# Four changes to PSUM banks and queue orders in a chain of four spectral layers

## What is computed

```python
xs  = rfft2(x)                                   # over both image axes
o1  = relu(xs @ w1 + b1)                         # complex, 8 blocks of 48 channels
o2  = softshrink(o1 @ w2 + b2, 0.01)             # real and imaginary part each
out = irfft2(o2) + x
```

## Time and profile before

| | |
|---|---|
| median of 3 runs | 2125.78 us |
| the profiled execution | 2123.25 us |
| its span, first to last instruction | 2121.5 us |
| mean granted TensorE clock | 0.978 of full speed |
| TensorE matmuls busy | 91% of the span |
| VectorE, ScalarE, GpSimd busy | 55%, 48%, 21% |

### The profile page before, as it was taken

One profiled execution on the slowest core, in us unless ns is written; L12 is line 12 of the kernel. 1 busy time (PEld: TensorE's weight loads), 2 busy tenths in 40 slices (PEclk: granted clock), 3 DMA queues, 4 the chain that ended last, 5 costly groups with the idle time before them and its releaser, 6 DMA issues.

```text
span 2121.5 us, 68757 instructions
## 1 busy us (share of the span) xinstructions
PE 1933.5 (91%) x31104; PEld 1592.9 (75%) x31104; DVE 1175.4 (55%) x2480; ACT 1012.2 (48%) x1644; POOL 439.9 (21%) x425
## 2 busy tenths in 40 slices
PE   5899984688998999999999999999799999999996
PEld 4677762566766999999999999999577777777774
DVE  3686887877855433333333333332566666666674
ACT  3655645566753333333333333333566555555652
POOL 3211103875621110000000000000311211212100
PEclk9999997799999999999999999999999999999999
DMA  9424727407435111111111111114804457257314
GB/s 166 90 48 81 126 53 137 62 4 126 96 84 132 30 30 30 30 30 30 30 30 30 30 30 30 30 30 71 140 3 89 70 96 124 49 81 126 62 30 93
DMA packets 299699, 141.03 MB, mean 66 GB/s; under 512 B 275760, under 2 KB 298032, under 8 KB 299440
## 3 DMA queue, kind: packets, MB, share of 16 engines
q1 hardware_dynamic: 299440, 137.08, 35.2%
HBM read 74.14 MB, written 62.91 MB: 65 GB/s over the span
## 4 chain that ended last, share of the span: by engine, by line
PE 73%; DVE 15%; ACT 6%; issue 3%; DMA 1%; SPq 1%; POOL 1%; DVEq 0%; POOLq 0%; ACTq 0%
PE ps L659 19%; PE ps L644 19%; DVE u L886 7%; PE ps L558 7%; PE ps L495 6%; PE ps L509 6%; PE ps L573 5%; PE ps L526 5%; PE ps L476 4%; ACT z L698 3%; DVE st L923 2%; DVE clamp L880 2%; PE ps L537 1%; DVE xs L911 1%; PE ps L629 1%
## 5 line engine op out<-in xcount | busy, mean ns | idle before, releaser
L1035 DVE TENSOR_TENSOR gl<-g,gh 128x512 fp32r<-128x512 f32 x192 | 156.7, 816 | 476.9 <-ACT gh L824 476.9
L886 DVE TENSOR_TENSOR u<-ps,clamp 64x192 f32<-64x192 f32 (+1 forms) x864 | 375.4, 434 | 27.8
L821 ACT ACTIVATE g<-ps,colp 128x512 f32<-128x512 f32 x192 | 132.5, 690 | 529.6 <-PE ps L644 529.6
L495 PEld LDWEIGHTS ps<-const,z 128*48 128x48 f32 x8384 | 269.5, 125 | 108.7 <-issue 100.9
L698 ACT ACTIVATE z<-ps 64x512 f32<-64x512 f32 x366 | 234.5, 641 | 106.7 <-PE ps L476 99.8
L495 PE MATMUL ps<-const,z 128*48 128x64 f32 (+1 forms) x8384 | 272.2, 218 | 8.9 <-issue 4.1
L1122 POOL COPY xn<-xs 128x512 f32<-128x512 f32 x144 | 151.4, 1090 | 569.4 <-PE ps L476 389.7
L659 PE MATMUL ps<-w2h,gh 128*128 128x384 f32 x768 | 261.9, 341 | 0.0
L659 PE MATMUL ps<-w2h,gl 128*128 128x384 f32 x768 | 258.6, 337 | 0.0
L659 PE MATMUL ps<-w2l,gh 128*128 128x384 f32 x768 | 257.5, 335 | 0.0
L509 PE MATMUL ps<-zf,w 112*64 112x512 f32 (+2 forms) x992 | 246.5, 569 | 9.8 <-ACT zf L718 9.7
(11 more groups left out here) (70 smaller groups left out, 2451.2 us busy)
## 6 DMA issues: line engine op xcount, KB each, us to landing
after<-xs SPq DMA_DIRECT2D x96, 384.0 KB, 5.4
xs<-after SPq DMA_DIRECT2D x94, 384.0 KB, 8.7
after<-om SPq DMA_DIRECT2D x32, 384.0 KB, 4.3
out<-xs SPq DMA_DIRECT2D x32, 384.0 KB, 5.4
xm<-after SPq DMA_DIRECT2D x30, 384.0 KB, 6.3
xs<-in_x SPq DMA_DIRECT2D x24, 384.0 KB, 8.8
wstage<-in_spectral SPq DMA_DIRECT2D x16, 210.0 KB, 5.9
xs<-in_x SPq DMA_DIRECT2D x4, 768.0 KB, 11.6
```

Source lines behind the costliest of these rows:

```text
L495: mm = pe.matmul(ps[a * SIDE:a * SIDE + BLOCK, F2_BANK, n * L.kh:(n + 1) * L.kh], z[:, g % 2, slot, :], basis(col + a * SIDE, L.kh), start ...
L886: dve.tensor_tensor(u[to, g % 2, :, start + b:start + size:BATCH], whole, limited, ALU.subtract).then_inc(u_ready, 1)
L1035: dve.tensor_tensor(gl[:, n % 4, :], g[:, n % 2, :], gh[:, n % 4, :], ALU.subtract).then_inc(g_low, 1)
```

## The change

- `m2` writes to banks 4 and 7 in turn, and waits for the group before the last in place of the last one. Since VectorE's scratch `clamp` is now no longer guarded by that wait, VectorE waits itself for its own four subtractions before it clamps again.
- `f6` writes to bank 6 alone, and waits for the eviction of the one before. Only in the drains does it go to banks 6 and 0 in turn.
- ScalarE's fourth piece of an `f1` stands behind the column eviction in place of ahead of it, in full layers and in the norm layer.
- At the head of the norm layer VectorE does its six pieces of the lead-in ahead of three `centre` calls, which were first.

```diff
-def spread_before(g):
+def spread_of(count):
+    return sum(layer_of(g).spread for g, _ in GROUPS[:count])
+def drains(g, k):
+    last = [b for _, b in SEGMENTS if g < b][0]
+    return g == last - 1 or g == last - 2 and k >= layer_of(g).first_rows
+def row_bank(g, k):
+    return 1 if drains(g, k) and k % 2 else 0
+def rows_to_clear(g, k):
+    n = ROWCHUNKS * g + k
+    earlier = [m for m in range(n) if row_bank(*ROW_CHUNKS[m]) == row_bank(g, k)]
+    return earlier[-1] + 1 if earlier else 0
...
-        F1_BANKS, F6_BANKS = (0, 1), (6, 7)
-        F2_BANK, M1_BANK, M2_BANK, F5_BANK = 2, 3, 4, 5
+        F1_BANKS, M2_BANKS, F6_BANKS = (0, 1), (4, 7), (6, 0)
+        F2_BANK, M1_BANK, F5_BANK = 2, 3, 5
...
 TensorE, m2
                 pe.wait_ge(h_ready, n + 1)
-                if n >= 1:
-                    pe.wait_ge(u_ready, spread_before(g) + L.spread * t)
+                if n >= 2:
+                    pe.wait_ge(u_ready, spread_of(n - 1))
+                bank = M2_BANKS[n % 2]
 (norm layer)
-                before = (g - BLOCKS) * L.n + t
-                if before:
-                    pe.wait_ge(u_imag, BATCH * before)
+                if imag_of(n - 1):
+                    pe.wait_ge(u_imag, imag_of(n - 1))
 TensorE, f6
-                if n >= 2:
-                    pe.wait_ge(res_ready, n - 1)
+                clear = rows_to_clear(g, k)
+                if clear:
+                    pe.wait_ge(res_ready, clear)
 ScalarE, spectral
+                        f2(g, t)
                         for k in late:
                             f1(g + 1, k, PIECES[3:4])
-                        f2(g, t)
 VectorE, m2 of full layers
+                    if groups_before(g) + t:
+                        dve.wait_ge(u_ready, spread_of(groups_before(g) + t))
                     dve.tensor_scalar(part, data, LAMBDA, -LAMBDA, ALU.min, ALU.max).then_inc(clamped, 1)
 VectorE, spectral
+                for k in range(TWINS):
+                    f1(first, k)
                 if norm:
                     for n in range(CHUNKS, CHUNKS + AHEAD):
                         centre(n)
-                for k in range(TWINS):
-                    f1(first, k)
```

More of the change, by code:

```diff
@@ L98, in groups_before, with imag_of @@
     return sum(LAYER[n // BLOCKS].n for n in range(g))
-def spread_before(g):
-    return sum(LAYER[n // BLOCKS].n * LAYER[n // BLOCKS].spread for n in range(g))
+GROUPS = [(g, t) for g in range(LAYERS * BLOCKS) for t in range(LAYER[g // BLOCKS].n)]
+def spread_of(count):
+    return sum(layer_of(g).spread for g, _ in GROUPS[:count])
+def imag_of(count):
+    return sum(BATCH for g, _ in GROUPS[:count] if layer_of(g).norm)
+def drains(g, k):
+    last = [b for _, b in SEGMENTS if g < b][0]
+    return g == last - 1 or g == last - 2 and k >= layer_of(g).first_rows
+ROW_CHUNKS = [(g, k) for g in range(LAYERS * BLOCKS) for k in range(ROWCHUNKS)]
+def row_bank(g, k):
[4 more added lines that the diff above has]
+    return earlier[-1] + 1 if earlier else 0
 def shrunk_before(g):
@@ L245, in build @@
         ps = ctx.enter_context(nc.psum_tensor("ps", [P, 8, 512], F32))
-        F1_BANKS, F6_BANKS = (0, 1), (6, 7)
-        F2_BANK, M1_BANK, M2_BANK, F5_BANK = 2, 3, 4, 5
+        F1_BANKS, M2_BANKS, F6_BANKS = (0, 1), (4, 7), (6, 0)
+        F2_BANK, M1_BANK, F5_BANK = 2, 3, 5
         LAST_BANKS = (F5_BANK, M1_BANK)
-        LEAD_BANKS = (F1_BANKS, F6_BANKS, F1_BANKS)
+        LEAD_BANKS = (F1_BANKS, (6, 7), F1_BANKS)
         TURN_BANKS, MM1_BANKS, MM2_BANKS = (6, 7), (4, 5), (0, 1, 2, 3)
@@ L525, in m2 @@
                         col = READY_SECOND if start + c < SPAN else MINUS
-                        mm = pe.matmul(ps[b * SIDE:(b + 1) * SIDE, M2_BANK, p * PAIR:(p + 1) * PAIR],
+                        mm = pe.matmul(ps[b * SIDE:(b + 1) * SIDE, bank, p * PAIR:(p + 1) * PAIR],
                                        h[0:ROWS, n % 2, c * SIDE:(c + 1) * SIDE],
@@ L536, in m2 @@
                         col = READY_SECOND + a * BLOCK
-                        mm = pe.matmul(ps[a * SIDE:(a + 1) * SIDE, M2_BANK, q * BLOCK:(q + 1) * BLOCK],
+                        mm = pe.matmul(ps[a * SIDE:(a + 1) * SIDE, bank, q * BLOCK:(q + 1) * BLOCK],
                                        h[0:ROWS, n % 2, q * SIDE:(q + 1) * SIDE],
@@ L548, in f5 @@
                         pe.wait_ge(s_const, 16)
-                    pe.wait_ge(u_ready, spread_before(g + 1))
+                    pe.wait_ge(u_ready, spread_of(groups_before(g + 1)))
                     if L.norm:
-                        pe.wait_ge(u_imag, BATCH * L.n * (g - BLOCKS + 1))
+                        pe.wait_ge(u_imag, imag_of(groups_before(g + 1)))
                     if L.norm and g % BLOCKS < 2:
@@ L568, in f6 @@
                     pe.wait_ge(v_ready, CHUNKS * (g + 1))
-                if n >= 2:
-                    pe.wait_ge(res_ready, n - 1)
+                clear = rows_to_clear(g, k)
+                if clear:
+                    pe.wait_ge(res_ready, clear)
                 rows = slice(k * ROWCHUNK, (k + 1) * ROWCHUNK)
                 for a in range(2):
-                    mm = pe.matmul(ps[a * SIDE:(a + 1) * SIDE, F6_BANKS[n % 2], 0:ROWCHUNK * BLOCK],
+                    mm = pe.matmul(ps[a * SIDE:(a + 1) * SIDE, F6_BANKS[row_bank(g, k)], 0:ROWCHUNK * BLOCK],
                                    basis(C_D6 + a * SIDE, SIDE), v[:, g % 2, rows, :].rearrange("p h c -> p (h c)"),
@@ L747, in m2 @@
                 act.wait_ge(m2_done, groups_before(g) + t + 1)
+                bank = M2_BANKS[(groups_before(g) + t) % 2]
                 start, size = L.groups[t]
@@ L751, in m2 @@
                     act.activation(u[HALF:SIDE, g % 2, :, start + b:start + size:BATCH],
-                                   ps[part, M2_BANK, 0:size // BATCH * BLOCK].rearrange("p (s c) -> p c s", c=BLOCK),
+                                   ps[part, bank, 0:size // BATCH * BLOCK].rearrange("p (s c) -> p c s", c=BLOCK),
                                    ACT.Copy).then_inc(u_imag, 1)
@@ L878, in m2 @@
                     pairs = size // BATCH
-                    part, data = clamp[:, 0:pairs * PAIR], ps[:, M2_BANK, 0:pairs * PAIR]
+                    part, data = clamp[:, 0:pairs * PAIR], ps[:, bank, 0:pairs * PAIR]
+                    if groups_before(g) + t:
+                        dve.wait_ge(u_ready, spread_of(groups_before(g) + t))
                     dve.tensor_scalar(part, data, LAMBDA, -LAMBDA, ALU.min, ALU.max).then_inc(clamped, 1)
@@ L889, in m2 @@
                 for b in range(BATCH):
-                    data = ps[b * HALF:(b + 1) * HALF, M2_BANK, 0:size // BATCH * BLOCK]
+                    data = ps[b * HALF:(b + 1) * HALF, bank, 0:size // BATCH * BLOCK]
                     dve.tensor_copy(u[0:HALF, g % 2, :, start + b:start + size:BATCH],
@@ L910, in f6 @@
                 to = residual(g, k * ROWCHUNK, ROWCHUNK)
-                dve.tensor_tensor(to, ps[:, F6_BANKS[n % 2], 0:ROWCHUNK * BLOCK].rearrange("p (h c) -> p h c", c=BLOCK),
+                dve.tensor_tensor(to, ps[:, F6_BANKS[row_bank(g, k)], 0:ROWCHUNK * BLOCK].rearrange("p (h c) -> p h c", c=BLOCK),
                                   to, ALU.add).then_inc(res_ready, 1)
```

## The result

The kernel after takes 2096.76 us (median of 4 runs, 2094.48 to 2098.42), the kernel before, run beside it, 2125.87 us (4 runs, 2122.17 to 2129.84). The ratio is 0.9862, with a 95% interval of 0.9841 to 0.9883: faster by 1.4%, 29 us, against a forecast of 21 us. The time lies inside the whole range (2089 to 2123) and 0.2 us outside the forecast's own, which begins at 2097. The profiled execution has a span of 2092.7 us at a mean granted clock of 0.975, against 2121.5 us at 0.978.

What follows compares the result with a forecast made beforehand. The prediction took TensorE's waits (73% of the chain), or VectorE's work where that is the chain, as the bound. Terms -24 - 8 + 14.2 - 2.9 = -20.7 us from 2125.78 gave 2105.1 us; whole range 2089 to 2123, its own 2097 to 2114.

Steps and rivals of the forecast that it cites:

- A border gains 1.37 of 1.69 us: Borders of two blocks, layers 2 and 3: 1.37 of 1.69 us of waits go; with the head, 24 us in all.
- my new wait before `f6`: At a border, `f6` with one bank waits for its eviction: 0.25 us come back.
- The 0.45 us at `zf`: At a border, the column eviction starts earlier, taking about 0.45 us off the first mix's 0.52 us wait for `zf`.
- Layer 0: Waits at block borders and VectorE's idle 1.07 us at the last exit go: 8 us gained, bounds 4 and 14.
- the second rival: Full layers: the wait moves to VectorE, gains of 11 not 24 and 4 not 8; 2122 us, chance 0.14.
- Norm layer, fourth piece: The piece, now behind the column eviction, delays the next `f1` by about 1.1 us: 14.2 us lost, bounds 0 and 20.
- the fourteen waits that I listed as signs: Norm layer: fourteen idle times of about 1.5 us before `f1` were to show in the changed trace.
- The first rival: Norm layer: the fourth piece costs nothing, the wait being the queue's own; 2091 us, chance 0.13.
- The small rival with 2096 us: A sum like the forecast's, with a larger gain in the norm layer's lead-in; near 2096 us, chance 0.05.
- Norm layer, lead-in: Head of the norm layer: VectorE stays the chain and gains 2.9 us, bounds 0 and 12.05.
- `f6` with one bank in the norm layer: The tightest place has 0.1 us to spare and TensorE comes later: costs nothing, at most 1 us.
- the third rival: Norm layer: new idle of about 1.5 us before eleven `f1` lowers TensorE's clock; slower, 2141 us, chance 0.08.

Runs made afterwards that it cites:

- runs 9 and 10: Reload of the norm layer's last residual pair cut to one eighth, in run 6's kernel (2082.42 us) and in the kernel before (2119.09 us).
- runs 1 and 5: Kernel after with ScalarE's fourth piece back ahead of the column eviction: in the norm layer alone (2089.60 us), and in all layers (2096.40 us).
- run 8: Kernel before with only `f6` changed, to one bank outside the drains: 2127.79 us, ratio 1.0012.
- run 2: Kernel after with the piece order and lead-in of the kernel before, so only the bank changes remain: 2100.55 us, ratio 0.9881.
- run 4: Kernel before with only VectorE's lead-in pieces put ahead of the three `centre` calls: 2123.05 us, ratio 0.9989.
- run 6: Kernel after, but in the norm layer the third and fourth piece both stand ahead of the activation: 2086.57 us, ratio 0.9812.

## Why the prediction was right, step by step

- **The bound, and which waits to count: right.** The earlier trace rows showed 22.1 us of waits for `u` and `zf` in layers 2 and 3 and 5.0 us for `u` at their head; these layers gave 25.6.
- **A border gains 1.37 of 1.69 us: undersized, 1.66 measured.** From the first `f1` of one block to that of the next, across a border, it took 36.96 us before and 35.32 after behind the border of the earlier trace rows, and 36.99 and 35.30 one block on. Take the start of the `f5` ahead of the border as zero (1558.67 before, 1552.60 after). The second mix of the short slot started at 5.13 and now at 3.57, 1.56 us earlier, where the brackets of the earlier trace rows had 1.17: some 0.4 us more. A bracket counts only from the printed end of the work ahead, while a mix that waits for nothing starts before that end (1553.53, with the `f5` ahead of it printed up to 1553.70). Of the 1.56 us 0.37 came back up to `f6` (1.54 us from that mix to `f6`, before 1.17), again without a bracket: 0.24 at the first mix, which starts 0.06 us after the end of the column eviction at 1556.87, and 0.13 at `f6`, which starts 0.05 us after the end of its eviction at 1557.66. So my new wait before `f6` was there, with half of its 0.25 us, and the other part I had not foreseen. `f6` gained 1.19 us, and I had 0.92. The 0.45 us at `zf` was right: from the `f1` to the first mix with 512 columns it took 5.16 us before and 4.70 after. The term was mis-sized because I read the waits from the brackets alone. Layers 2 and 3 gave 25.6 us against 24: their head, up to the border of the earlier trace rows, 2.9 where I had 4.7, with 4.0 us of new stalls of the kind of runs 9 and 10 (at 1500.42, 1513.57 and 1519.77), and the rest 22.7 where I had 19.3. By runs 1 and 5 the order of the pieces is 6.8 us of the gain of the full layers, where I had 0.45 us a border, some 9 with layer 0.
- **Layer 0: -8 forecast, -6.2 measured.** The idle 1.07 us of the earlier trace rows is gone: VectorE's clamp at 164.20 follows its subtractions (162.04 + 2.06) at once. But there part of the wait moved, as the second rival had it for the full layers: from 20 to 365 us TensorE waited 9.4 us for `xs` before and 14.5 after, in 16 places in place of 7, where it had waited 18.4 us for `u`. The nine new places, 3.9 us, lie in the blocks with `bn_stats` or right behind them, where the prediction has VectorE as the bound. It takes both edits: with `f6` in one bank alone (run 8) it is 9.4 us still, with two banks for the second mix as well (run 2) 14.6. In layers 2 and 3 that rival fell: 1.0 us before `f6`. By the other traces (above) the 6.2 us are no firmer than my 8.
- **Norm layer, fourth piece: +14.2 forecast. The mechanism was right to the tenth, the net was half.** The slot above took 1.11 us more from the start of the column transform to `f1` (457.94 - 454.85 = 3.09, before 463.94 - 461.96 = 1.98), against 1.1 forecast, and a block took 32.25 us (first `f1` at 440.91, the next block's at 473.16) against 29.65 (449.11, 478.76): 2.6 us, which is 2 x 1.1 + 0.42. The column eviction of slot 3 waits 0.39 us for `f2`, forecast 0.4, and the copy behind it comes later by that. Of the fourteen waits that I listed as signs eleven are there; the first three `f1` wait for VectorE (1.54, 2.87 and 2.27 us). From the first `f5` to the MLP, TensorE's waits at the start of an `f1` grew by 12.3 us and those for ScalarE's `v` by 2.5, together 14.8. What I hadn't in the sum is that the stalls without a releaser inside groups of matmuls, 9.6 us in 8 places there (4.30 and 2.94 the longest), became 2.4 us in 3: 7.2 us back. 14.2 - 7.2 = 7.0, measured 7.3 from trace to trace, and 5.5 to 7.2 by run 1. The 4.3 us stood in the earlier trace rows as the longest of the 13, and the sum gave it no term.
- **The first rival (the piece is free) fell**: undone, the move gave 5.5 to 7.2 us. Its 2091 us lay 6 us from the result and my 2105 lay 8, but for another reason, the stalls. The small rival with 2096 us fell too, though its number came out: it wanted a larger gain in the lead-in, and that gave 0.9 us more than forecast. That the whole came out inside the range owes something to luck, since the term that I had left out was a third of the forecast gain.
- **Norm layer, lead-in: -2.9 forecast, -3.8 from trace to trace**, -4.1 by runs 2 and 5, -4.1 alone by the medians and -2.3 by the ratio (run 4, whose interval reaches to no change). Counted from the first `f1`, the third starts after 5.2 us, where I had 5.3, and the `centre` calls after 8.3 us, where I had 8.7. That is 0.4 of the 0.9 us; the rest was not traced.
- **`f6` with one bank in the norm layer: nothing, right.** Run 8 has it for the whole kernel.
- **The clock: the third rival fell.** From 396 to 600 us the mean granted clock is 0.95, before 0.97. In stretches of 10 us from 426 to 606 us it is 1.00, but for 0.93 and 0.73 from 506 to 526, where an idle of 1.48 us and the stall of 1.76 us follow each other. So the idle of 1.50 us before an `f1` alone didn't bring it to the lower level; behind the 3.73 us stall of run 6 it was 0.50, the lower level, from 510 to 515.
- **"No further gain"**, which the Trainium skill reports of a second set of PSUM buffers in a matmul kernel (TensorE: Matmul & The Clock Gate, HAM oscillation), doesn't carry over: banks alone gave 26.6 us. The section doesn't say what bounded that kernel; here TensorE waited for that one bank, at borders and at the heads of segments.
- **The sum.** -25.6 - 0.5 - 6.2 + 7.3 - 3.8 = -28.8 against -20.7: of the 8.1 us, 6.9 are the norm layer behind its head, where the stalls had no term, 1.6 layers 2 and 3, 0.5 the MLP, and 0.9 the lead-in, less 1.8 in layer 0.

The best version (run 6) keeps the banks, the lead-in and the full layers' order, and in the norm layer puts both late pieces where they end before `f2`: 2086.57 us, 1.9% under before and 0.5% under after.

## What to carry to other kernels

A second bank is worth what TensorE waits for that bank on the path, and it can be had from a stage whose eviction mostly has time (here it hadn't in nine places of layer 0, 3.9 us): sum the waits, and look at the borders, where the stages that fill the gaps are missing. An order that helps one form of a loop can hurt another by the same amount, and a total of zero hides both: where stages stand in other slots, cost the edit for each form and keep it where it pays. Before a wait is charged in full, look for stalls near it that the delay can run into.

## What was unexpected of the hardware

TensorE stood still inside a run of 64 equal matmuls, with no semaphore named, for 3.73 us (run 6) and 4.30 us (before), at the same matmul of the code for each. The stalled matmul started 1.62 and 1.66 us after a 16 KB packet of the instruction queue had ended, and so did, at 1.19 to 1.79 us, all 140 stalls of this kind over 0.8 us in the twelve traces. When a transfer of 3.1 MB over the same time was cut to an eighth, the stall fell to 0.99 and 0.88 us, and the granted clock rose to 1.00 from 0.69 over 10 us in run 6. With the smaller reload the kernel before took 8 us less by the medians and 6 by the ratio (2126.95 against 2119.09), more than the stall itself; VectorE's wait for the reload went with it. For run 6 it is some 4 us (2086.57 against 2082.42), which lie within the intervals.
